# Attention value products of two neighbouring tiles issued together, with six tile buffers instead of five

## The reference

```python
x = x + 0.5 * ffn(layernorm(x))      # ffn(z) = z @ W.T + b + (z @ V_r) @ C.T, 256 -> 256
x = x + attn(layernorm(x))           # 16 heads of 16 features
x = x + 0.5 * ffn(layernorm(x))

# attention, per head
att = (q @ k.T) / sqrt(16)           # causal mask
att = where(att > 0, att**2 + 1, where(att >= -100, 1 - att / 100, 0)) / 1000
y   = att @ v                        # then y @ W_proj
```

## Time and profile before

| | us |
|---|---|
| median of three runs | 2101.22 |
| lowest, highest | 2091.39, 2101.42 |
| the profiled execution | 2099.58 |
| its span (first to last instruction) | 2097.9 |

### The profile page before, as it was taken

The page is one execution under the profiler, slowest core; times in us unless marked ns, Lnnn a source line. Parts: engine busy times, 40 slices in busy tenths (PEclk is TensorE's granted clock), DMA queues, the critical chain, the costliest instruction groups (busy, mean ns, idle before and its releaser), DMA issues.

```text
span 2097.9 us, 34607 instructions
## 1 busy us (share of the span) xinstructions
PE 1790.7 (85%) x12694; PEld 769.2 (37%) x12694; DVE 1344.5 (64%) x2225; ACT 1351.3 (64%) x1474; POOL 1112.9 (53%) x1067
## 2 busy tenths in 40 slices
PE   4777789898989889898988989898888888888885
PEld 3544334243434333343433334343333223233334
DVE  2466667676766666676666667666666767676652
ACT  1244467777776767667676766667676777776651
POOL 3243446566565647466564646656464546464552
PEclk9899889999999999999999999999999999999997
DMA  2343331423333241333324143332314122322111
GB/s 79 123 130 109 118 107 51 111 71 97 86 89 112 60 128 43 106 92 90 118 61 128 37 111 94 87 107 75 105 47 118 56 74 65 76 59 86 56 33 54
DMA packets 155053, 181.06 MB, mean 86 GB/s; under 512 B 22012, under 2 KB 129660, under 8 KB 152836
## 3 DMA queue, kind: packets, MB, share of 16 engines
q1 hardware_dynamic: 154884, 178.82, 29.3%
HBM read 102.43 MB, written 76.30 MB: 85 GB/s over the span
## 4 chain that ended last, share of the span: by engine, by line
PE 60%; DVE 19%; issue 10%; ACT 7%; DMA 2%; POOL 2%; SPq 0%; DVEq 0%; ACTq 0%; POOLq 0%
PE y_ps L941 23%; PE score L941 18%; PE bank L941 16%; DVE rp L876 10%; DVE lin L882 3%; ACT rp L805 2%; PE bank L960 2%; ACT rp L791 1%; POOL z L671 1%; ACT rp L797 1%; DVE qk_max L888 1%; DVE bnst_ln L901 1%; DVE rest L440 1%; ACT zT L753 1%; DMA part_scratch<-parts 1%
## 5 line engine op out<-in xcount | busy, mean ns | idle before, releaser
L876 DVE TENSOR_SCALAR rp<-score 128x1024 f32<-128x1024 f32 (+3 forms) x896 | 887.1, 990 | 391.3 <-PE score L941 389.5
L941 PE MATMUL score<-qs,ks 96*128 96x512 bf16 (+3 forms) x2560 | 683.3, 357 | 177.2 <-DVE lin L882 92.7
L690 POOL TENSOR_TENSOR rp<-rp 128x1024 f32<-128x1024 f32 x320 | 605.1, 1894 | 229.9 <-DVE rp L876 228.9
L791 ACT ACTIVATE rp<-score 128x1024 f32<-128x1024 f32 x384 | 393.0, 1024 | 494.9 <-PE score L941 493.6
L941 PE MATMUL y_ps<-rp,vt 128*16 128x512 f32 (+3 forms) x5120 | 610.3, 549 | 5.8 <-ACT rp L805 4.6
L805 ACT ACTIVATE rp<-rp,rise 128x1024 f32<-128x1024 f32 (+1 forms) x384 | 488.7, 1286 | 0.0
L696 POOL TENSOR_SCALAR_AFFINE_SELECT rp<-rp 128x512 f32<-128x512 f32 x256 | 162.3, 634 | 555.5 <-DVE rp L876 551.9
L941 PEld LDWEIGHTS score<-qs,ks 96*128 96x128 bf16 x2560 | 209.0, 99 | 565.0 <-DVE rp L876 303.8
L797 ACT ACTIVATE rp<-rp 128x2048 f32<-128x2048 f32 (+3 forms) x256 | 323.7, 1265 | 23.1 <-POOL rp L696 22.9
L882 DVE SCALAR_TENSOR_TENSOR lin<-score,slope_mask 128x256 f32<-128x256 f32 x512 | 212.1, 414 | 0.0
L941 PE MATMUL bank<-w_ffn,zT 128*128 128x256 f32 x512 | 169.2, 428 | 17.2 <-ACT zT L753 17.2
(11 more groups left out here) (76 smaller groups left out, 1259.4 us busy)
## 6 DMA issues: line engine op xcount, KB each, us to landing
part_scratch<-parts SPq DMA_DIRECT2D x16, 1536.0 KB, 5.8
qs<-part_scratch SPq DMA_DIRECT2D x384, 64.0 KB
ks<-part_scratch SPq DMA_DIRECT2D x384, 64.0 KB, 2.3
state_scratch<-st_new SPq DMA_DIRECT2D x16, 528.0 KB
st<-state_scratch SPq DMA_DIRECT2D x64, 132.0 KB
x_sb<-in_L_attn_x_dram SPq DMA_DIRECT2D x16, 512.0 KB, 4.3
x_scratch<-x SPq DMA_DIRECT2D x16, 512.0 KB, 5.3
qT_scratch<-qkT SPq DMA_DIRECT2D x16, 512.0 KB, 3.6
```

The source lines that it names most:

```text
L690: pool.tensor_tensor(half, half, half, ALU.mult).then_inc(squared["pool"], 1)
L791: nc.scalar.activation(rp[T % RP_BUFS][:, 2:4, :], score[H % S_BUFS][:], ACT.Relu).then_inc(raised["act"], 1)
L876: nc.vector.tensor_scalar(rp[T % RP_BUFS][:, 2 * u:2 * u + 2, off:CH], score[H % S_BUFS][:, :, off:CH], 0.0, RISE if is_diag(T) or pool_sq ...
L941: return nc.tensor.matmul(*args, start=start, stop=stop, skip_group_check=True)
```

## The change

Two things are edited. `RP_BUFS` becomes 6. And the slot of a tile's values is taken from `behind = T + 1 - T % 2 + LAG`: for an odd T that is T + 3 as before, for an even T it is T + 4. So the values of tiles T (even) and T + 1 stand one behind the other in the slot of the first half of tile T + 4, which is the place where those of T + 1 stood before; the slot between holds none. The rest of the program is placed as it was.

```diff
-S_BUFS, RP_BUFS, L_BUFS = 2, 5, 5
+S_BUFS, RP_BUFS, L_BUFS = 2, 6, 5
...
     for T in range(ITERS * NT):
-        s = slot[2 * (T + LAG)] if T + LAG < ITERS * NT else o.drain + T + LAG - ITERS * NT
-        o.values[s] = T
+        behind = T + 1 - T % 2 + LAG
+        s = slot[2 * behind] if behind < ITERS * NT else o.drain + behind - ITERS * NT
+        o.values.setdefault(s, []).append(T)
         o.values_slot.append(s)
...
-                if s in o.values:
-                    values(o.values[s])
+                for T in o.values.get(s, ()):
+                    values(T)
```

## The result

| | before | after |
|---|---|---|
| median, us | 2097.28 (4 runs) | 2229.06 (4 runs) |
| lowest, highest, us | 2091.39, 2101.42 | 2219.33, 2235.12 |
| ratio to before, 95% interval | | 1.0626 [1.0576, 1.0676] |
| span of the profiled execution, us | 2097.9 | 2217.5 |
| mean granted clock | 0.956 | 0.940 |

The kernel is 6.3% slower, 132 us by the medians and 120 us by the two profiled spans. The forecast was 99 us. The profiled execution after the change is the fastest of its four; the other three are 9 to 16 us longer, at a clock of 0.935 to 0.937.

What follows compares the result with a forecast made beforehand. TensorE was taken as bound by waits for score buffers and its own timeline, values covering the buffers' way round. New waits less savings gave +2, +26, +30 and +41 us, sum +99: 2200 us, range 2095 to 2270.

Steps and rivals of the forecast that it cites:

- Step 2: Off-diagonal pair without jobs: halves wait for raises, 4.75 us a pair against 3.90, 1.09 added; 0.23 with three job pieces.
- Step 1: Fewer switches into and out of values groups: 4.9, 5.4, 4.5 us saved an iteration (1 to 3, 4 to 11, 12 to 15).
- The rule on weight loads: TensorE pulls weight loads ahead of running matmuls: a switch costs nothing, saving 0, time some 80 us above the sum.
- Step 3: Pairs with a diagonal tile, 12 of 20 an iteration: 0.7 us added each, bounds 0.33 and 1.1.
- Step 4: Iterations 4 to 11: about five pairs, bound by longer chains on DVE or ACT, already wait and add nothing.
- the mark set for it: Third chunk, iterations 4 to 11: Step 4 is wrong if the wait of 2.48 us is gone or has grown.
- Rival C: New waits lower TensorE's clock in iterations 1 to 15: 2245 or 2290 us; chance 0.08 of ending above 2270.
- The stretches: Growth by iterations: 0, +2 us; 1 to 3, +26; 4 to 11, +30; 12 to 15, +41.
- the last stretch: Iterations 12 to 15, few jobs: +10.3 us each, +41 in all; the whole is wrong if they are not longer.
- Iteration 0: Its 80 halves are spread over 172 slots with jobs between: +2 us.
- The other edits: Sixth buffer, later key and query loads, copies of `y_ps` unchanged: priced at 0.
- The sign that was set at 150 us or more: TensorE's idle time before score halves up from 174 us by 150 or more, with ACT's raise among the releasers.

Runs made afterwards that it cites:

- Runs 7 and 8: Every raise cut to 128 queries, squares over constants, six buffers: in the order of before 1919.06 us (0.9172), in the changed order 1945.13 us (0.9288).
- run 9: The kernel before with a slot's job piece ahead of its values instead of behind them: 2079.73 us, 0.9926.
- run 5: The changed kernel with values together only where both tiles at that place are off-diagonal (6 of 20 places): 2150.48 us, 1.0273.
- run 6: The changed kernel with up to two needless 256-column matmuls before O1, the odd tile's second half, where job pieces are missing, iterations 1 to 15: 2184.24 us, 1.0432.
- runs 1 and 2: The kernel before with six rp buffers alone, 2092.3 us; then also all values one tile later, singly, last-stage loads at most 9 slots ahead, 2093.31 us.
- run 10: The kernel before with six buffers and needless 512-column matmuls ahead of five long waits in iterations 4 to 11: 2084.22 us, 0.9944.
- run 11: The kernel before with job pieces ahead of values (except slot 0), six buffers and needless matmuls at long waits of iterations 4 to 11: 2052.72 us, 0.9791.
- run 12: As run 11, with needless matmuls also in iterations 1 to 3: 2048.38 us, 0.9787.

## Why the prediction came out as it did

The direction and the mechanism were right: the values groups were the cover of the way round of a score buffer, and four halves without one wait for their raises. The size was a quarter too small by the medians, 99 us against 132. The term that was mis-sized is the clock, which the sum put at nothing; it is worth up to 41 us. The waits less the savings come to 79 us or somewhat more in the profiled spans, less than the forecast 99. So the forecast was nearer than its terms deserved: two errors partly cancelled. Point by point:

- **Step 2, the price of a pair.** Right to 0.01 us where it was worked out: 4.74 us against 4.75, with 0.69 us of idle before O1 (forecast about 0.8) and ACT's raise among the releasers. Runs 7 and 8 show that it is the raises: with short ones a pair without `lin` takes 3.94 us.
- **Step 1, the saving.** Right in its parts: 1.84 us for two values groups is 0.86 + 0.98, not 2 x 0.98. But in the dense pair it bought nothing. The forecast had 5.7 us, the trace 5.86, since E2 waits for DVE and the saved time only ends in that wait.
- **The rule on weight loads.** By what step 1 cites from the Trainium skill (TensorE: Matmul & The Clock Gate, Step-by-step: what each phase is for), a switch would have cost nothing. The trace doesn't agree with that: the saving is there (1.84 us, and run 9's 0.09 us a tile). Which of the rule's two conditions fails here no run shows.
- **Step 3, diagonal pairs.** Right in sum: 14 places with 69 to 75 us by the difference of run 5 to the whole, forecast 71. The price of 0.7 us a pair was not measured by itself.
- **Step 4, what already waits.** Wrong, but for less than the stretch suggests. Iterations 4 to 11 were to grow by 30 us and grew by 50.6; at most 12 of the 20 us too many are clock, so 8 or more are waits that were not swallowed. By the mark set for it, the wait of 2.48 us is gone as such. Its chunk is 2 us shorter, but not because the new waits were swallowed: idle time rose from 5.6 to 7.3 us, and the clock from 0.91 to 1.00. In the next chunk 1.36 us became 2.34, the 1.49 us stayed, a wait for ACT's `zT` went from 0.64 to 1.34, and with the clock behind them the chunk is 4.8 us longer. In run 5 the off-diagonal places cost 3.5 us an iteration here, not 0.6, of which 22.0 / 8 = 2.7 are idle time.
- **A slip in the sum.** Step 4 leaves three of the six off-diagonal pairs of iterations 4 to 11, and the sum prices four. With three it would have been 2 to 7 us lower. It also takes 56 filled slots in iteration 11 and 18 in iteration 15; by the order table both have 44. Neither matters.
- **Rival C, the clock.** "Which by these rows the clock survives" was wrong. The forecast looked at one stretch with waits up to 1.3 us at full clock and took it as true of all. The mean clock fell by 0.016, at most 41 us, and run 6, which fills gaps, gives back 1.9%, some 40 us. The rival had priced a loss of 0.03 at 45 us and given all above 2270 us a chance of 0.08.
- **The stretches without the clock.** Against a forecast of 2, 26, 30 and 41 us the stretches grew by 12, 21, 51 and 36. Less at most 9, 1, 12 and 15 us of clock these are 3, 20, 39 and 21. So the last stretch, which was said to have the fewest unknowns, was priced far too high for its waits and came out near its number by luck: iterations 13 and 14 of run 6, at a clock of 1.00, are 106.9 and 107.9 us against 99.9 and 101.5, +6.7 on average where the sum had +10.3. Without the fillers they are 109.5 and 115.6 us, +11.9 on average. In run 5, too, the 3.1 us an iteration in 1 to 3 fit the forecast of 3.7 by luck, since most of them are clock.
- **Iteration 0.** +2 was forecast, +12 measured, of which some 3 are the shift of the window's edge. The clock there is 0.87 against 0.91 before, which can be up to 9 us. It was not tested by itself.
- **The other edits.** Zero, as priced: runs 1 and 2.
- **The sign that was set at 150 us or more.** It was not met: idle before score halves grew by 127. The rows count the tail of a matmul's result as busy (a score half lasts 0.60 where the next product can start after 0.43), so about 0.17 us of each wait is not in the idle time. That is an estimate; with 390 waits instead of 238 it makes up the difference.

What stays open: why fillers and job order together gain 2.1% when alone they gain 0.6 and 0.7 (in iterations 4 to 11, where the kernel before takes 972.7 us at a clock of 0.97, run 9 takes 961.1 at 0.97, run 10 961.2 at 0.99 and run 11 934.6 at 1.00, so part of it is clock); and why of iterations with the same instructions some lose clock and some don't. Two such after the change, iterations 5 and 7:

```profile
807.20:935.00 127.80, 106.69 (x794) 48.12 (x792) 81.97 (x135) 84.41 (x94) 71.56 (x69) 0.97 0.30 88
1064.50:1197.00 132.50, 111.39 (x794) 49.50 (x793) 81.88 (x135) 84.39 (x94) 71.49 (x69) 0.94 0.28 85
```

## What to carry to other kernels

Before work is bunched in the engine that bounds, count what that work covers: here a score buffer needs 1.75 to 1.95 us to come back, and a tile's products took just as long. A switch that costs 0.2 us is worth saving only where more than a buffer's way round of other work remains between two uses of the buffer. And a wait of TensorE has a second price, the clock behind it: price it from several stretches of the trace, and where a wait can't be removed, try to fill it.

## What the runs showed of the hardware

- Behind waits of 1.3 and 2.3 us in a stretch of TensorE with further gaps, the granted clock of the next products was 0.52 and 0.68, that is, for most of them the lower of the two levels. The same happened behind shorter ones: in iteration 14, behind gaps of 0.69 and 0.45 us, 16 values matmuls lasted 3.49 us instead of 1.91.

```profile
1984.95 0.60 PE L943 MATMUL score<-qs,ks 96*128 96x512 bf16 x2 [0.69 <-ACT rp L793]
1986.01 0.59 PE L943 MATMUL score<-qs,ks 96*128 96x512 bf16 x2 [0.45 <-DVE lin L884]
...
1987.48 3.49 PE L943 MATMUL y_ps<-rp,vt 128*16 128x512 f32 x16
```

- Such gaps don't always cost the clock. In iteration 13 the same two stand before the same products, and these run at full speed (1877.54, 1.91 us, shown above). What decides between the two cases these rows don't show.

```profile
1875.07 0.61 PE L943 MATMUL score<-qs,ks 96*128 96x512 bf16 x2 [0.69 <-ACT rp L793]
1876.13 0.59 PE L943 MATMUL score<-qs,ks 96*128 96x512 bf16 x2 [0.45 <-DVE lin L884]
```

- Needless products paid: 1.9% in the changed kernel, and 1.3% on top of the new place of the jobs (2079.73 to 2052.72 us), with iterations at a clock of 1.00. In iterations 1 to 3 they did little: 2.6 us in run 6, nothing in run 12.
